# First layer: five low parts at equal distances among GpSimd's 64 scatters

## What is computed

```python
x = L0_attn_hidden_states
xn = _layernorm(x, axis=-1)
x = x + _L0_attn_ref(xn, ...) + _L0_ffn_ref(xn, ...)
xn = _layernorm(x, axis=-1)
x = x + _L1_attn_ref(xn, ...) + _L1_ffn_ref(xn, ...)
```

## Time and profile before

| what | us |
|---|---|
| median of 3 runs | 1163.87 |
| lowest, highest | 1162.66, 1164.16 |
| the profiled execution | 1159.85 |
| its span in the profile | 1158.0 |
| attention of the first layer, about | 97 to 233 |

### The profile page before, as it was taken

How to read it: one execution, slowest core, us unless ns; L and a number is a source line. 1 busy time by engine, 2 the same in 40 slices (tenths; PEclk the granted TensorE clock), 3 DMA queues, 4 the chain that set the end, 5 groups by cost and what they waited for, 6 DMA issues and landing times.

```text
span 1158.0 us, 17535 instructions
## 1 busy us (share of the span) xinstructions
PE 1023.2 (88%) x5780; PEld 747.3 (65%) x5780; DVE 765.2 (66%) x1591; ACT 604.8 (52%) x911; POOL 317.8 (27%) x331
## 2 busy tenths in 40 slices
PE   4997896678999938699999999999999996999996
PEld 3876775467999934455554555555555565888885
DVE  6575444546665525889889888888888836444338
ACT  6324444246565643356665666666666665444431
POOL 2005578026674430000000021221220000455442
PEclk9999899779999978699999999999999998999999
DMA  6862233244544344111121113222222115333243
GB/s 225 322 265 113 90 110 125 97 136 128 157 128 131 121 191 164 18 28 28 21 36 28 28 49 62 56 68 45 68 60 50 62 35 185 103 100 110 88 187 145
DMA packets 49140, 120.49 MB, mean 104 GB/s; under 512 B 7752, under 2 KB 24904, under 8 KB 48520
## 3 DMA queue, kind: packets, MB, share of 16 engines
q1 hardware_dynamic: 36096, 82.80, 24.9%
q0 software_dynamic: 11808, 32.37, 7.4%
q10 hardware_dynamic: 1152, 4.19, 0.9%
HBM read 72.30 MB, written 52.42 MB: 108 GB/s over the span
## 4 chain that ended last, share of the span: by engine, by line
PE 69%; DVE 17%; ACT 4%; issue 3%; DMA 3%; another core or an unknown queue 2%; POOL 1%; SPq 0%; ACTq 0%; DVEq 0%; POOLq 0%
PE psum L806 10%; PE psum L827 9%; PE psum L815 7%; DVE work_f L1688 5%; PE psum L536 5%; PE psum L622 5%; PE psum L538 4%; PE psum L537 4%; PE psum L623 4%; PE psum L624 4%; PE psum L608 3%; PE psum L633 2%; PE psum L654 1%; PE psum L655 1%
## 5 line engine op out<-in xcount | busy, mean ns | idle before, releaser
L1688 DVE TENSOR_REDUCE work_f<-psum 128x1 f32<-128x512 f32 x512 | 337.3, 685 | 48.8 <-PE psum L806 46.1
L806 PE MATMUL psum<-work_r 128*128 128x512 f32 x512 | 207.9, 445 | 18.8 <-DVE work_f L1688 7.0
L1192 ACT ACTIVATE work_f<-psum 128x1024 f32<-128x1024 f32 x172 | 169.5, 1023 | 104.7 <-PE psum L815 99.8
L473 POOL DMA_INDIRECT yk<-yb,dest x134 | 131.2, 979 | 238.8 <-ACT yb L1046 209.4
L806 PEld LDWEIGHTS psum<-work_r 128*128 128x128 f32 x512 | 93.4, 190 | 133.6 <-DVE work_f L1688 72.8
L815 PE MATMUL psum<-qm,work_r 128*128 128x512 f32 x512 | 160.8, 396 | 0.9 <-ACT work_f L1192 0.8
L466 POOL DMA_INDIRECT xg<-xn,slot x112 | 108.2, 966 | 181.4 <-PE psum L842 143.0
L815 PEld LDWEIGHTS psum<-qm,work_r 128*128 128x128 f32 x512 | 93.7, 188 | 24.2 <-ACT work_f L1192 6.3
L622 PE MATMUL psum<-wexp,xbh 128*128 x268 | 102.7, 383 | 6.3 <-issue 6.1
L1192 ACT ACTIVATE pt<-psum 128x1024 f32<-128x1024 f32 x84 | 82.8, 1024 | 45.8 <-PE psum L815 42.7
L623 PE MATMUL psum<-wexp,xbh 128*128 x268 | 96.6, 360 | 0.0
(11 more groups left out here) (218 smaller groups left out, 2077.5 us busy)
## 6 DMA issues: line engine op xcount, KB each, us to landing
xb<-xg SPq DMA_DIRECT2D x67, 258.0 KB
xg<-in_pad SPq DMA_DIRECT2D x1, 10320.0 KB
yg<-yk SPq DMA_DIRECT2D x20, 512.0 KB, 9.0
stage<-in_moe SPq DMA_DIRECT2D x16, 608.0 KB
xg<-in_pad SPq DMA_DIRECT2D x1, 7224.0 KB
work_r<-work_r SPq DMA_DIRECT2D x128, 48.0 KB
work_r<-work_r SPq DMA_DIRECT2D x32, 192.0 KB
stage<-in_moe SPq DMA_DIRECT2D x16, 384.0 KB, 4.2
```

The lines of the kernel that those rows point to most:

```text
L473: nc.gpsimd.indirect_dma_start(yk[l], bass.IndirectOffsetOnAxis(ap=dest[:, j % 8, i:i + 1], axis=0), yb[l][:, j % 2, i, :], None).then_inc ...
L806: nc.tensor.matmul(next_bank(pe, ("scores", n), b_mx, n + 1), qs[g % 2][:, t * P:(t + 1) * P], km[g % 4][:, r, :], start=True, stop=True). ...
L1192: nc.scalar.activation(pt[((b * NG + g) * QT + t) % 3][:, 2 * h:2 * h + 2, :], psum[:, 3 + 2 * h:5 + 2 * h, :], ACT.Exp, scale=float(HD) * ...
L1688: v.reduce_max(mx[:, s % 2, i:i + 1], ring["scores", n], AX.X).then_inc(b_mx, 1)
```

## The change

One line: the scatters ahead of which the five low parts stand.

```diff
-            early = {16: 0, 20: 1, 24: 2, 44: 3, 48: 4}
+            early = {10: 0, 21: 1, 32: 2, 43: 3, 54: 4}
             for n in range(TT * TOP0):
                 if n in early:
                     low_expert(early[n])
                 dispatch(0, n)
```

## The result

On the chip of the first measurement the changed kernel takes 1145.62 us (median of 4 runs, 1144.26 to 1148.19) against 1163.26 for the kernel before (median of 4, 1159.66 to 1164.16), a ratio of 0.9864 with an interval of 0.9842 to 0.9887. The forecast was 1142. The profiled execution took 1145.10, with a span of 1143.3 us, 14.7 less than that of the kernel before, whose profiled execution (1159.85) was near its fastest (1159.66).

What follows compares the result with a forecast made beforehand. It took TensorE's signals, held late under unbroken rows of GpSimd scatters in first-layer attention, as the loss to cut. Batch gains 9 + 1 + 12 + 0 = 22 us from 1163.87 gave 1142 us, range 1132 to 1163.

Steps and rivals of the forecast that it cites:

- hold: A matmul has ended by TensorE's row, but the engine waiting for its semaphore starts much later.
- the rival: Holds come from TensorE's own stretches or only from profiling, not scatters; only L1582's 2.7 us return, 1161 us; chance 0.17.
- First batch, 9 us forecast: First attention batch: hold ends at 110.1 to 111.7 instead of 117.74, gaining 7 us, plus 2 us of TensorE clock.
- Second batch, 1 us forecast: Second attention batch: L1582 returns 2.7 us, less 1.7 us for a late signal under a row of eleven scatters.
- The bound of 3 us: Second batch: a signal at the end of the row of eleven scatters may be late by 0 to 3 us.
- The rival with four long rows: Four rows of 10 or 11 scatters over all batches cost up to 36 us; 6 us slower, 1170 us; chance 0.11.
- Third batch, 12 us forecast: Third attention batch: holds of 16.5 us go, less 4.4 us for maxima held and L1582 perhaps meeting low part 3.
- Fourth batch, nothing forecast: Fourth attention batch: 2 us lost to a hold under the last ten scatters against 2 us of clock returned.
- The signs that were named: Later profile: ScalarE waits under 4 us, L1582 0.5, third addition within 2 us, unknown queue 1% or less, last addition near 210.
- the two signs of being wrong: Holds of 5 us or more inside rows of ten and eleven, or ScalarE waiting for expert 7's load.
- from 7 to 10 us on, released 1 to 3 us after the row: Holds build up 7 to 10 us into an unbroken scatter row and end 1 to 3 us after it pauses.
- the floor behind low part 4: Expert 7's load lands at 188, 5 us before ScalarE asks; a fourth batch beginning before 180 would wait.

Runs made afterwards that it cites:

- e7_by_ten: Changed kernel with the low parts ahead of scatters 10, 20, 30, 40 and 50; 1146.36 us, 0.9872 of the kernel before.
- e11_halves_no_floor: Changed kernel, low parts halved and spread earlier, expert 7's high part moved behind the transposed-probability copies; 1130.93 us against 1160.68 for the kernel before.
- e12_narrow_again: Kernel before with first-layer scatters of 16 columns instead of 258, into their own tensor; 1159.25 us beside 1160.68 for the kernel before.
- e6_after_again: Changed kernel run again unchanged, where holds occurred; 1145.08 us, 0.9861 of the kernel before.
- e1_first_only: Kernel before with only the first low part moved, from ahead of scatter 16 to 10; 1130.51 us, ratio 1.0005, no holds.
- e5_before_again: Kernel before run again unchanged, where holds occurred; 1159.0 us (one run), median 1160.98 beside it.
- e4_four_pauses: Changed kernel plus idle GpSimd powers ahead of scatters 5, 26, 37 and 59; 1141.06 us, 1.0096 of the kernel before, without holds.
- e2_last_only: Kernel before with only the last low part moved, from ahead of scatter 48 to 54; 1133.24 us, ratio 1.0025, no holds.

## Why the prediction was right, point by point

**The cause.** The prediction laid the waits that ended remote to unbroken rows of scatters. `e7_by_ten` (a hold under the lengthened row), `e11_halves_no_floor` (no wait that ended remote, with rows of at most 6 ahead of the last 11) and `e12_narrow_again` (holds kept where only bytes changed) bear out, on chips that have holds, that how GpSimd's scatters are broken up sets the holds. The first half of the rival, that they belong to TensorE's own stretches, does not fit `e11_halves_no_floor`, in whose first three batches TensorE has the same work. The second half, that they exist only while the profiler records, is not excluded. A pause between scatters is also a pause in what there is to record, the scatters of 64 bytes leave as many updates to record, and records are missing in every set that has holds. The prediction's argument against it was that the profiled execution is faster than the median without a profile. But every execution that the experiments list has a span and a granted clock, so none of them is known to have run unrecorded. The Trainium skill ("SBUF — State Buffer", section "Who interferes with whom") says that PE never waits on anyone. The traces don't contradict it for memory ports: in the hold before 175.11 of the kernel before, TensorE's matmuls go on every 0.23 us, and only the news of their end comes late. TensorE stops where it needs what the held engine makes, as in the 9.35 us before 208.56.

**First batch, 9 us forecast.** 136.47 became 128.31, with the scatters beginning 0.5 us earlier, so 7.7. The hold ended at 110.30, inside the 110.1 to 111.7 of the working, and the clock came back in full. 1.7 us went to a new hold at its end: the last matmul ended at 126.34 + 0.28 = 126.62, the addition started at 128.31. That signal fell 5.4 us into a row of only five scatters, where the prediction's table has no hold.

**Second batch, 1 us forecast, 6.4 us lost.** This term failed. L1582 did return its 2.7 us. But the row of eleven that now lies over this batch was priced at 1.7 us from the row of 8, and the batch took 35.1 us, 9.0 more than the hold-free 26.1. Of these, 3.4 us are the addition's late signal (160.00 to 163.40), under the next row of eleven, and 5.6 us had been lost before, by the late transposes. Some 1.5 us of the 5.6 are clock: TensorE idled 4.05 us for what VectorE makes behind the copies, its clock was 0.59 in 148 to 152, and eight of its matmuls there follow each other every 0.43 us instead of 0.23:

```profile
148.09 0.51 PE L536 MATMUL psum<-work_r 128*128 128x512 f32 x1 [4.05 <-DVE work_r L1589]
```

```profile
148.00:152.00 4.00, 3.91 (x11) 3.04 (x12) 0.04 (x1) 0.37 (x1) 3.08 (x4) 0.59 0.73 249
```

The bound of 3 us was for a single late signal in a batch, where each late one delays all that follow. The rival with four long rows had 10 us for each row of eleven; here 9.0 us came from two such rows together.

**Third batch, 12 us forecast.** 42.1 became 28.6, 13.5 us. The total is near, the parts are not: the working left 3 us for the maxima and nothing for the end, since the batch was to end with low part 4. It began at 163.40 instead of 155, its maxima followed low part 3 without a hold, and its end fell 6.5 us into the last row of ten, where the signal was 2.1 us late (189.91 to 192.02). Low part 3 met no L1582, for the same reason.

**Fourth batch, nothing forecast.** 24.7 became 26.2, so -1.5. The working set 2 us for a hold against 2 us of clock. The clock gave nothing back (0.80 in 192 to 218, 0.79 over this batch before). The first scores were done at 190.88 + 0.39 = 191.27, and their maximum started at 195.55. This hold of 4.3 us stands under TensorE's name and not as remote, so the absence of "remote" is not by itself the absence of a hold; the lengths of the batches are the safer sign:

```profile
190.88 0.39 PE L538 MATMUL psum<-work_r 128*128 128x512 f32 x1
```

```profile
195.55 0.69 DVE L1575 TENSOR_REDUCE work_f<-psum 128x1 f32<-128x512 f32 x1 [2.31 <-PE psum L538]
```

**Sum.** 7.7 - 6.4 + 13.5 - 1.5 = 13.3 us in the profiled pair, 0.5 from the earlier start of the scatters and 0.9 behind the attention, together 14.7; the medians differ by 17.6. The forecast sum was 22, and the 7 that the profiled pair lacks are the second batch. That the median came within 3.6 us of 1142 is in part luck: the forecast set the sum against a median that lay 4.0 us above the profiled execution, and the difference of the medians is 2.9 us larger than that of the two executions whose parts are known.

**The signs that were named.** Low part 1 no longer waits, the longest L1582 of the second batch takes 0.57 us, and the unknown queue has 1%, as forecast. ScalarE's wait before 110.30 is 4.29 us, just over the 4, and the third addition starts 2.1 us after the last matmul, just over the 2. The last addition comes at 218.23, not near 210. And one of the two signs of being wrong did come: a signal was held for 6.6 us inside the row of eleven over the second batch (139.52 to 146.13), and in `e6_after_again` that for the second addition for 6.1 (158.05 to 164.13). Several signals also came while scatters still ran, without a pause (141.84 and 192.02 here, 111.43 already in the earlier trace rows). So the rule "from 7 to 10 us on, released 1 to 3 us after the row" is too simple, though breaking the rows up does help.

**What the prediction did not see** is that its table held only where holds occur. Its rival "1161, holds not made by the scatters" asked whether the holds were real, but nothing in one trace could show that the same kernel runs 30 us faster elsewhere. There the floor behind low part 4, named with 5 us to spare, becomes the deciding term, for the fourth batch then begins at 177 and not at 185.

## What to carry to other kernels

A wait that the profile can't name, repeated in one stretch, deserves to be laid beside what another engine streams in that stretch; here it was long under unbroken rows of scatters and vanished with short pauses. Work that GpSimd has to do anyway makes such pauses without extra time, if it is cut small, and if what waits behind each piece (here the staging of the next expert) is not pushed late. Before trusting a gain of 1%, look at the same pair on a second chip: this change is 1.4% faster where there are holds and 0.3% slower where there are none.

## What the runs showed of the hardware

- The kernel before takes 1161 to 1163 us in three of the five measurements (on two chips at least) and 1130 us in the two others, on two more chips. Most of the difference lies in the first layer's attention, whose last addition starts at 232.0 with holds; in `e1_first_only`, which keeps the kernel's time, it starts at 198.3 without.
- With holds, TensorE works on until it needs a held engine's result, and the updates of its matmuls' semaphores arrive late and can then come in a bunch: in the kernel before, six within 0.4 us at 175.1 to 175.5, for matmuls that ended between 168.1 and 175.1.
- Holds do not go with bytes: scatters of 64 bytes a row instead of 1032 keep them (207.25 against 207.29 for the third addition).
- A `TENSOR_SCALAR` over 128x512 in SBUF takes 3.1 to 3.4 us instead of 0.49 when it begins within 0.2 us of a low part on GpSimd (0.74 and some 2.3 us, two subtractions in a row). It happened in the kernel before (3.17, and 3.21 in `e5_before_again`), in `e12_narrow_again` (3.13), in `e4_four_pauses` (3.18) and in `e2_last_only` (3.40).
- Left open: what of the scatters builds a hold up (their number, rows or updates), whether any pause ends one or only a low part, what makes one chip or occasion have them and another not, and whether a hold exists when nothing is recorded. No time here is known to be that of an unrecorded execution, and the traces with holds lack 7 of 10 of the scatters' updates.
